# Attention on one core: the order of maxima, score and value groups in TensorE's program

## What is computed

```python
# x, ctx: (16, 256, 256); 16 heads of 16 columns
x = x + tanh(g_xattn[0]) * decayed_scan(layernorm(x), ctx, ctx)       # step 1
x = x + tanh(g_ffn[0]) * fp4_ffn(layernorm(x), w_gate, w_up, w_down)  # step 2
# step 3: attention, q = layernorm(x), k = v = ctx
q = q * cos + rotate_half(q) * sin          # per head
k = k * cos + rotate_half(k) * sin
scores = einsum('bqhd,bkhd->bhqk', q, k) / sqrt(16) + slope[h] * (key - query)
attn = softmax(scores, axis=-1)
x = x + tanh(g_xattn[1]) * einsum('bhqk,bkhd->bqhd', attn, v)
x = x + tanh(g_ffn[1]) * bfp_ffn(layernorm(x), w_fc, b_fc, w_proj, b_proj)  # step 4
```

## Time and profile before

| | |
|---|---|
| three executions | 856.55, 862.73, 863.42 us; median 862.73 us |
| the profiled execution | 860.34 us, of which the profile's span is 858.2 us |
| busy, share of the span | PE 83%, DVE 83%, ACT 57%, POOL 50% |
| layer 0 | to about 380 us |
| attention | about 380 to 697 us |
| last feed-forward step | from about 697 us to the end |

### The profile page before, as it was taken

How to read it: one execution, slowest core, us unless ns; L and a number is a source line. 1 busy time by engine, 2 the same in 40 slices (tenths; PEclk the granted TensorE clock), 3 DMA queues, 4 the chain that set the end, 5 groups by cost and what they waited for, 6 DMA issues and landing times.

```text
span 858.2 us, 16571 instructions
## 1 busy us (share of the span) xinstructions
PE 713.5 (83%) x5090; PEld 517.0 (60%) x5090; DVE 708.5 (83%) x1230; ACT 488.0 (57%) x939; POOL 431.1 (50%) x331
## 2 busy tenths in 40 slices
PE   2255999999999998779999999999999775777775
PEld 1255888887888877556565555656565333444444
DVE  6867788998889887868898989898888658888885
ACT  3433545445454342337777777777778674555553
POOL 4524565555655545644444554555443526655553
PEclk8576999999999999879999999999999987888898
DMA  8800000000000000010000000000001000100011
GB/s 279 246 3 0 1 1 1 0 0 0 0 0 1 1 1 1 1 50 2 3 2 2 1 1 1 2 1 1 1 1 50 2 1 1 37 25 24 26 37 50
DMA packets 17719, 18.35 MB, mean 21 GB/s; under 512 B 1670, under 2 KB 16912, under 8 KB 17680
## 3 DMA queue, kind: packets, MB, share of 16 engines
q1 hardware_dynamic: 17084, 17.66, 6.4%
q10 hardware_dynamic: 596, 0.20, 0.1%
HBM read 13.39 MB, written 4.19 MB: 20 GB/s over the span
## 4 chain that ended last, share of the span: by engine, by line
PE 33%; DVE 30%; issue 16%; POOL 9%; ACT 8%; DVEq 1%; DMA 1%; POOLq 1%; ACTq 0%; SPq 0%
PE a_ps_t L561 7%; PE a_ps_m L579 6%; DVE maxima L1497 5%; PE a_ps_pv L615 4%; DVE f_ps_small L1582 4%; PE a_ps_s L600 3%; POOL hs L1110 3%; PE ps_o L522 3%; DVE hup L1324 2%; DVE f_hcode L1598 2%; DVE yup L1293 2%; POOL xres L1090 2%; DVE hscale L1318 2%; ACT hmag L866 1%; PE a_ps_pv L623 1%
## 5 line engine op out<-in xcount | busy, mean ns | idle before, releaser
L1497 DVE TENSOR_REDUCE maxima<-a_ps_m 128x2 f32<-128x512 f32 x256 | 166.3, 687 | 35.4 <-PE a_ps_m L579 34.7
L919 ACT ACTIVATE probs<-a_ps_s 128x512 f32<-128x512 f32 x256 | 149.2, 602 | 42.3 <-PE a_ps_s L600 40.1
L579 PE MATMUL a_ps_m<-stack_t 64*128 64x256 f32 x512 | 107.5, 328 | 19.9 <-DVE maxima L1497 16.7
L579 PEld LDWEIGHTS a_ps_m<-stack_t 64*128 64x128 f32 x512 | 68.3, 188 | 78.7 <-DVE maxima L1497 49.5
L600 PE MATMUL a_ps_s<-stack_t 64*128 64x256 f32 x512 | 100.0, 308 | 3.7 <-ACT probs L919 2.9
L1141 POOL TENSOR_TENSOR stack<-roped,stack 128x512 f32<-128x512 f32 x32 | 42.6, 1333 | 116.8 <-DVE stack L1487 115.3
L491 PE MATMUL ps_gu<-w1h,yth 128*128 128x352 f32 x256 | 88.6, 346 | 13.2 <-DVE h L1311 13.2
L522 PE MATMUL ps_o<-w2t,hqt 128*128 128x256 f32 (+1 forms) x384 | 97.9, 390 | 0.2 <-ACT hqt L851 0.2
L615 PE MATMUL a_ps_pv<-probs,v_aug 128*32 128x256 f32 x1024 | 83.0, 396 | 2.9 <-ACT probs L919 2.5
L910 ACT CAST stack_t<-a_ps_t 128x512 fp32r<-128x512 f32 x128 | 70.9, 588 | 24.5 <-PE a_ps_t L561 23.7
L561 PE MATMUL a_ps_t<-idf,stack 128*128 128x128 f32 x512 | 77.2, 294 | 9.0 <-POOL stack L1141 4.6
(11 more groups left out here) (176 smaller groups left out, 1613.3 us busy)
## 6 DMA issues: line engine op xcount, KB each, us to landing
xres<-in_x SPq DMA_DIRECT2D x16, 256.0 KB, 3.2
ctx<-in_ctx SPq DMA_DIRECT2D x16, 256.0 KB, 3.8
out_x<-f_y SPq DMA_DIRECT2D x16, 256.0 KB, 2.1
w1a_raw<-in_w_gate_up SPq DMA_DIRECT2D x1, 1024.0 KB, 6.2
w_raw<-in_w_fc SPq DMA_DIRECT2D x1, 1024.0 KB, 5.7
w_raw<-in_w_proj SPq DMA_DIRECT2D x1, 1024.0 KB, 5.0
w_raw<-in_w_down SPq DMA_DIRECT2D x1, 704.0 KB, 9.3
stack_t<-neg_max_t SPq DMA_DIRECT2D x32, 8.0 KB
```

The lines of the kernel that those rows point to most:

```text
L579: ins = nc.tensor.matmul(a_ps_m[:, half, n, :], a_stack_t[b.par][rows, 0, pair, c * P:(c + 1) * P], a_stack_t[b.par][rows, 1, pair, :], st ...
L919: nc.scalar.activation(a_probs[:, u % 8], a_ps_s[:, u % 2], ACT.Exp).then_inc(a_exp, 1)
L1497: nc.vector.tensor_reduce(a_maxima[:, b.par, c, 4 * quad + half:4 * quad + half + 3:2], a_ps_m[:, half], X, ALU.max).then_inc(a_v_max, 1)
```

## The change

The loop over m in TensorE's body is written anew. A third score group, S2, stands ahead of the loop. M(m) is then followed by S(m+3) for every m up to 12, so that a maxima group and the score group behind it have different `half`. V(g) comes after the score group of m = 2g+1, that is behind S(2g+4) instead of S(2g+3); for g = 6 it follows M13, and V7 follows M15. In the last batch V7 so comes ahead of `ff_fc`, and what stands at m = 8 and m = 12 comes behind S11 and S15 instead of behind V3 and V5. No instruction is added or taken away, and no wait is changed.

```diff
-                u = 0
                 for g in range(6, TG):
-                    at_scores(b, u)
+                    at_scores(b, g - 6)
                     if nxt:
                         at_turn(nxt, g)
-                    u += 1
+                at_scores(b, 2)
                 for m in range(MU):
                     if nxt:
                         at_scores_for_max(nxt, m)
-                    if m % 8 != 7:
-                        at_scores(b, u)
-                        u += 1
-                        if u % 2 == 0 and u >= 4:
-                            at_times_v(b, (u - 4) // 2)
+                    if m + 3 < SU:
+                        at_scores(b, m + 3)
+                    if m % 2 == 1:
+                        at_times_v(b, m // 2)
                     if not nxt and m == 8:
                         turn_w34(2)
                         turn_w34(3)
...
-                at_times_v(b, PG - 1)
                 if nxt:
                     at_turn_max(nxt)
```

## The result

| | median (lowest to highest), us | ratio to the kernel before |
|---|---|---|
| the kernel before | 862.56 (856.55 to 863.42) | |
| the changed kernel | 874.07 (872.46 to 874.59) | 1.0147, 95% interval 1.0110 to 1.0183 |

The change makes the kernel slower by 11.5 us in the medians. Of the profiled executions the spans are 871.9 and 858.2 us. One execution of the changed kernel (1563.34 us) and one of an experiment (two ahead, flipped: 988.59 us, with the granted clock at 0.65 on average) were far longer than all the others and enter no comparison.

A forecast was written before the change was run, and what follows sets the result against it. DVE was taken to bound each body's maxima stretch, PE's program the rest up to M0. Thirteen bodies at +0.26 (3.4) plus 0.8 - 0.5 + 1.5 gave +5.2 us, hence 868 us, range 861 to 875.

The forecast's parts named there:

- Ahead of the loop, +0.24: Before each body's loop: S2 takes M0's place, so the first maximum starts 0.24 us later, uncovered.
- The first value group, and the rest of the loop: V0 and M2 wait behind S4: DVE stalls 0.7 us, 0.33 lost; later waits of 0.1 to 0.4 at V3, V5.
- The sum for a body, +0.26: One full attention body, all its parts together: the turn of the maxima at 516.12 instead of 515.86, +0.26 us.
- The rule on strict program order: By the skill's rule, three or four value groups a body would win about 0.2 us each; the forecast followed the trace instead.
- reading (c): Where PE has work waiting, the order of neighbours makes no difference, as each half runs through its own groups.
- The first body, +0.8: First body: M0 waits behind S2, which waits for exponent 0, and DVE has no slack; +0.8 us.
- The last body with maxima, -0.5: Last body with maxima: V4 is done ahead of the stretch at the lower clock; -0.5 us.
- The last batch, +1.5: Last batch: S10 ahead of V3 waits for exponent 8, delaying the turned weights and ACT's copy; +1.5 us, uncovered.
- V7 ahead, -0.1: Last batch: V7 ahead of two products instead of behind them gives back about 0.1 us.
- ACT as the pacer: In the bodies' loop, ACT's chain of score groups and exponents sets the pace instead of DVE: 874 us; chance 0.15.
- the stalls pay for the front: Vanished stalls offset the front, last batch's delay hidden: body 0 to 0.1 us, whole 0 to +3, 863 to 866; chance 0.17.
- the kernel gets faster: DVE runs through its maxima without a pause, a body wins up to 0.69 us: 855.5 or 854 us; chance 0.10.

The follow-up runs named there:

- two ahead, flipped: Kernel before with S(m+2) behind every M(m) in the bodies and maxima groups on the other head, making neighbours opposite halves; 857.03 us, ratio 0.9959.
- all six orders: Body orders of the kernel before, the changed kernel, and four follow-ups: only S2 in front, S(m+2) with equal or opposite halves, and a recurrence-found one; 851.27 to 874.07 us.
- new bodies alone: The new order in the 15 bodies with a next batch, the last batch as in the kernel before; 868.22 us, ratio 1.0111.
- filled behind V0 to V4: Four idle transposes behind each of V0 to V4 in the last batch: old bodies with new last batch, 867.27 us; recurrence-found bodies with old last batch, 856.09 us.
- flipped pair: Kernel before with S(m+2) behind every M(m) in the bodies, neighbours of equal halves or of opposite halves; 863.73 and 857.03 us.
- front-only kernel: The kernel before with only the third score group, S2, put ahead in the bodies, last batch as before; 864.16 us, ratio 1.0037.
- filled pair: Old bodies with 38 idle transposes in three gaps where PE stood still, with the new and the old last batch; 861.61 and 857.96 us.
- fitted order: Kernel before with a body order found by the recurrence (M0, M1 first, value groups later), old last batch; 851.27 us, ratio 0.9904; again 854.02 us, 0.9915.

## Why the prediction was off, step by step

- **What bounds the kernel.** Right. DVE's stretch and PE's program up to M0 add up to a body in all six orders, and orders that only move DVE's waits move the time.
- **Ahead of the loop, +0.24.** Right: +0.23 measured alone, 1.24 instead of 0.99 us ahead of the first maximum.
- **The first value group, and the rest of the loop.** Right in place and nearly in size: 0.65 us of stall (0.7), the third maximum 1.94 us behind the first (1.93 by the recurrence), the fifth 3.22 (3.21), and the sixteenth starts 11.76 us behind it (11.72).
- **The sum for a body, +0.26.** Measured +0.39, so 13 of them cost 5.0 and not 3.4 us. The term is 0.13 too small. A part of that is in its own sum: by the ends of the last maximum (516.07 and 515.77) it is +0.30, and only by the turns (516.12 and 515.86, where the trace has 515.83) +0.26. The rest is that the stretch of the maxima grew by 0.14 us, from 12.30 to 12.44, where 0.06 was forecast; between the stretches it is the forecast front, 0.25.
- **The rule on strict program order.** The Trainium skill ("TensorE: Matmul & The Clock Gate", Part 3, The mechanism) says that matmuls start in strict program order. The trace of the changed kernel does not agree either: its program has S2, M0, S3, two matmuls each, and three score matmuls have started, from 505.42 on, when the first of M0 does at 505.76. The flipped pair shows that neighbours' halves do matter, by 0.5 us a body, where groups are released one at a time. My reading (c), that they don't where work waits, also fits: the recurrence built on it gives both.
- **The first body, +0.8.** +1.0 with the new bodies alone, where the low clock in this part is as long as before (5.2 and 5.3 us). In the changed kernel's own profile it is +1.8, with 7.7 us of low clock in it.
- **The last body with maxima, -0.5.** It is 0.3 us shorter from its first to its last maximum (15.15 against 15.47). But the clock stayed low until 684.1, past the last maximum's end at 680.4, and exponent 0 of the last batch started 5.5 us behind that end instead of 4.1.
- **The last batch, +1.5. This step failed.** It measured +8.2. The chain was one of the places, and the right one (exponent 8, S10, V3, S11, weights, copy, exponent 10): ACT waited 3.10 us in it, where 1.5 to 2 was forecast and 0.53 stood before. But the sum held this one wait and V7's 0.1 us, nothing else, and took the clock of the kernel before as given. It priced V3 and S11 at the higher level; its 1.07 us from the weights to the copy came from a row at the lower one (it is 0.65 at the higher, in both kernels that were filled behind V0 to V4). What it put at nothing without a reason is everything else in this batch: 2.7 us ahead of exponent 9, 1.8 from exponent 10 to 15 and 1.5 from there to the reciprocal. With the same filling, the order costs 3.6 us; the rest is gone there, and the low clock is 10.2 instead of 30.7 us long. So the low clock is the likely cause of the rest, and no run varies the clock alone. The closing sentence of the prediction named a falling clock as what would make it wrong, and said that nothing prepares for it. But the kernel before had the lower level in this very batch:

```profile
686.10:689.50 3.40, 3.40 (x32) 2.24 (x28) 2.42 (x8) 2.87 (x5) 1.04 (x2) 0.50 0.01 2
678.00:698.00 20.00, 16.07 (x130) 8.72 (x131) 9.80 (x37) 16.15 (x31) 4.84 (x6) 0.91 0.01 2
```

Its idle PE (busy 16.07 of 20.00 us) looks like a second sign, but is not one that decides: in the front-only kernel PE was busy for 16.91 of the 22.00 us from 678 to 700, at a clock of 1.00 throughout.
- **V7 ahead, -0.1.** Right: with V7 behind the products, the reciprocal comes 0.14 us later from exponent 15 on.
- **The rivals.** ACT as the pacer did not come. ACT's waits for score groups did shrink, but its waits for value groups (the row `pv_t` further up) grew by as much: 32.1 and 9.1 us before, 41.2 in all, and 16.8 and 24.0 now, 40.8 in all. So ACT stands still as long as before. And PE's matmuls of score groups waited for an exponent in the loop only once in a body (12 waits, 3.5 us, in the twelve bodies), at S4, not at every pair. The rival that the stalls pay for the front fell too, and so did the one that the kernel gets faster: M2 was held by S4, as the prediction said would decide it.

```profile
ACT probs L919 <- PE a_ps_s L600: 32.1, 76, 0.7
ACT pv_t L925 <- PE a_ps_pv L615: 9.1, 12, 0.8
```

```profile
ACT probs L916 <- PE a_ps_s L600: 16.8, 57, 0.5
```

- **The chances.** 871.4 us or less had 0.80, and the time is above. The terms that make the difference are the last batch (6.7 us more than forecast) and the bodies (1.6 more).

**What stays open.** What begins a stretch of low clock, and how long it lasts. Kernels with the same last batch, unfilled, had from 3.4 to 20.5 us of it. All five with the new last batch unfilled had 20 us or more behind the last maximum, and none of the seven with the old one. That is an association over twelve profiles, each of one execution. In all five the low stretch began 5 to 7 us behind the last maximum, far ahead of the weights, so the longer wait for the weights cannot have begun it. Whether the 3.6 us of the filled pair would shrink to my 1.5 at a clock that is high throughout could not be tried, since the filling did not keep it high.

## What to carry to other kernels

Lay a hand-written order out group by group, with durations from the trace, before changing it. A recurrence that hits the old trace to 0.05 us gave the sign and nearly the size of five new orders and found one about 0.9% faster, where a rule of thumb (pair opposite halves) was right about the pairing and wrong about the whole. Price separately the batch that runs under other conditions (the last one, with other work mixed in), and at both clock levels. In such a batch a delay priced at one wait can cost several times that: here 1.5 us was forecast, 3.6 measured with the gaps filled and 8.2 without.

## What the runs showed of the hardware

- Matmuls that use opposite halves of the rows overlap, and each half runs through its own groups, also past a group of the other half that stands ahead in the program. Opposite neighbours instead of equal ones, with the order kept, took the stretch of 16 maxima from 12.64 to 12.11 us.
- The same last batch, instruction for instruction, ran with 3.4 to 20.5 us of low clock around it in seven different kernels, and its reciprocal came at 22.33 to 26.46 us. A value group takes 0.64 us at the higher level and 1.08 at the lower, 16 bf16 transposes 1.07 and 1.89.
- 38 idle transposes in gaps took 4.8 us off one kernel, 1.3 off another and nothing off the fitted order. Twenty of the same kind in front of awaited work gave 1.0 us in one and cost the fitted order 1.8 to 4.6, by which of its two runs is taken.
